# Expert slots of a mixture-of-experts layer on one core: more input buffers, another order of evacuation, and gathers further ahead

## The chip, the core and the metric

The kernel is one program on one core of a Trainium2 chip. It works with TensorE (PE, matrix products and transposes), ScalarE (ACT), VectorE (DVE), GpSimd (POOL) and SyncE (SP, which here only issues transfers). The metric is the device time of one execution in microseconds, the median of several runs.

## What is computed

A block of gated cross-attention (x plus tanh(g) times attention of the normalised x over a context) followed by a gated mixture-of-experts layer, on 2048 tokens of width 512, all in float32. The change touches the second part only:

```python
logits = xt @ router_w + router_b
scores = softmax(logits) + router_bias
# the best two of four groups of experts, and in them the best two of 16 experts
gate = zeros((T, E)).at[arange(T)[:, None], idx].add(vals)

def step(y, p):
    w1, b1, w2, b2, w3, b3, ge = p                 # 512x128, 512x128, 128x512
    h = silu(xt @ w1 + b1) * (xt @ w2 + b2)
    return (y + ge[:, None] * (h @ w3 + b3), None)
y, _ = scan(step, zeros_like(xt), (ew1, eb1, ew2, eb2, ew3, eb3, gate.T))
z = silu(xt @ sw1 + sb1) * (xt @ sw2 + sb2) @ sw3 + sb3     # a shared expert, for all tokens
x = x + tanh(g_ffn) * (y + z)
```

## The kernel before

Products are made from float32 operands split into a high and a low part, each held as fp32r: `three_pass` (lines 82 to 86) issues high by high, low by high and high by low. So each operand is first rounded to its high part on ScalarE and then subtracted into its low part on VectorE.

The three stages run one after the other: keys, values and normalised tokens; attention; the mixture of experts. In the third, each token goes to two experts only. The pairs of token and expert are sorted by expert into **slots** of 256 rows of one expert; there are at most 31 of them (`SLOTS`), and all 31 are run, whether they are filled or not. For slot s:

- SyncE loads the expert's weights into `w_raw[s % 2]` (`load_w`, lines 1522 to 1532): w1 and w2 (L1530), then w3 (L1532). It waits until the low parts of slot s-2 are made from that buffer, then reads the expert's number.
- GpSimd gathers the slot's 256 rows of the normalised x into `rows_in[s % 2]`, in two indirect transfers (`gather`, L1608), and later scatters its 256 rows of output from `y_out[s % 2]` to memory in two more (`scatter`, L1618). Its order is written out without a loop: gather s, then scatter s-4. Before the gather of slot s it waits for the transposes of s-2, before a scatter for `y_out`. Rows of empty places are skipped by a bounds check.
- TensorE's order in slot s (`slot`, in the tensor block) is: transpose the rows of slot s+1 (L2033); the product `up` of slot s, 24 matmuls of 256 columns into `ps_up`; the product `down` of slot s-1, 6 matmuls of 512 columns into `ps_down`.
- ScalarE's order in slot s: xs_hi of s+1 (L1696, two halves), the high part of w1 and w2 of s+1 (L1702), silu of s (L1728), h_hi of s (L1733), `evacuate` of s-1 (L1717: two halves of `ps_down`, scaled by the gate, into `y_out`), the high part of w3 of s+1 (L1708). Each half of `evacuate` waits for its product and for the scatter of s-3, which read the same `y_out`.
- VectorE's order in slot s: xs_lo of s+1 (L1902), the low part of w1 and w2 of s+1 (L1907), a copy of the two columns of biases of s+1 into `biases` (L1909), whose end is the signal `w_up_lo_made` for `up`; then h_sb of s (L1925: `up` plus bias, times silu), h_lo of s (L1928), the low part of w3 of s+1 (L1914).

`over_slots` (lines 1457 to 1465) runs slots 0 to 3 as straight code, slots 4 to 27 in a loop with two slots in its body, and the last three as straight code. SyncE, ScalarE, VectorE and TensorE go through it; GpSimd has no loop.

Around the slots: the shared expert's `up` products run before them and its `down` products after them. Buffers are placed by hand, some on top of others: `x_hi` and `x_lo`, which the shared expert's `up` reads, share their memory with buffers used after it. When the last scatter has landed, the 16 blocks of expert outputs are loaded back (`y2`, L1541) into buffers that are free by then, `rows_in` and `w_raw` among them, added, and stored.

Of the kernel before, what the change touches and what calls it, by code (L numbers as in the profile page):

```python
# [42 lines left out]
E = 16  # L43
# [23 lines left out]
def f32(ap):  # L67

    return ap.bitcast(F32)
# [370 lines left out]


# [773 lines left out]
def stage_three(nc, a, common, scratch, out):  # L1215
# [12 lines left out]
    with ExitStack() as stack:  # L1228
        b = Buffers(nc, stack)
        with ExitStack() as after_up:  # L1230
            e = Buffers(nc, after_up)
            h = []
            for o in range(OCTETS):
# [22 lines left out]
        biases = [b.sb(f"biases{i}", [P, 2]) for i in range(2)]  # L1256
# [20 lines left out]
        w_raw = [b.sb(f"w3_raw{i}", [P, 3, 512]) for i in range(2)]  # L1277
        rows_in = [b.sb(f"rows_in{i}", [P, 2, D]) for i in range(2)]
# [87 lines left out]
        y2_pairs += [buf[:, 0:2] for buf in (*rows_in, *w_raw)]  # L1366
# [48 lines left out]
        x_in = [b.sem(f"slot_x_in{i}") for i in range(2)]  # L1415
        w_in = [b.sem(f"slot_w_in{i}") for i in range(2)]
# [39 lines left out]

        def over_slots(eng, slot):
# [44 lines left out]
        def _(sp):  # L1502
# [19 lines left out]
            def load_w(s, r):  # L1522
                if late(s, 2):

                    sp.wait_ge(w_up_lo_made, s - 1)
                    sp.wait_ge(w_down_lo_made, s - 1)
                column = slice(s, s + 1) if isinstance(s, int) else bass.ds(s, 1)
                e = sp.value_load(moe["slot_expert"][0:1, column], min_val=0, max_val=E - 1)
                for i, name in enumerate(("L0_ffn_ew1", "L0_ffn_ew2")):
                    sp.dma_start(w_raw[r][:, i].rearrange("p (c n) -> p c n", c=C),  # L1530
                                 a[name][e].rearrange("(p c) n -> p c n", c=C)).then_inc(w_in[r], 16)
                sp.dma_start(w_raw[r][:, 2], a["L0_ffn_ew3"][e]).then_inc(w_in[r], 16)  # L1532
# [16 lines left out]
        def _(pool):  # L1549
# [52 lines left out]
            def gather(s):  # L1602
                r = s % 2
                if s >= 2:

                    pool.wait_ge(turned, 2 * s - 2)
                for half in range(2):
                    pool.indirect_dma_start(  # L1608
                        out=rows_in[r][:, half], out_offset=None, in_=xn,
# [524 lines left out]
```

## Time and profile before

| | us |
|---|---|
| median of 3 runs | 1537.16 |
| lowest and highest | 1534.63, 1537.56 |
| the profiled execution, its own time | 1544.32 |
| its span, first to last instruction | 1542.6 |
| busy in the span: PE | 1470.0 |
| DVE | 973.8 |
| ACT | 779.0 |
| POOL | 188.0 |

The profile records one execution. The page gives for each engine the busy time and the number of instructions. Other views are tables of busy time in chosen stretches, groups of instructions by line, sums of waits, and timelines of one engine. L1702 is line 1702 of the kernel; L84 to L86 are the three lines of `three_pass`, so its products are told apart by their tiles: `bank<-xs_hi,w_hi` is `up`, `bank<-w_hi,h_hi` is `down`. In a timeline the columns are start, duration (of all, where several are merged as x2), engine, line, operation, tiles, and, in brackets, how long the engine stood idle before it and what released it. "issue" is a release that the profile can't put down to another engine's signal, "remote" one by an unknown sender. Durations of neighbouring ScalarE and VectorE instructions overlap a little, so start to next start is the time that one costs. A group of lines gives busy time and mean ns of one, then idle time before the group and its releasers.

### The profile page before, as it was taken

The page shows a single profiled execution, that of the slowest core. Times are in us where ns is not written, and L with a number is a line of the kernel's source. Part 1 is how long each engine was busy: PE and PEld are TensorE (multiplying, and loading weights), DVE is VectorE, ACT ScalarE, POOL GpSimd, SP SyncE. Part 2 cuts the span into 40 slices and gives each one's busy share as a digit, 9 for nine tenths or more (in the row PEclk, how much of TensorE's full clock was granted, in tenths as well). Part 3 has the DMA queues.
Part 4 walks back from the last instruction along what each step waited for, and adds up shares of the span by engine and source line. Part 5 has one row for each costly group of instructions (what it writes and reads, how often), then busy time and mean ns, then how long its engine had stood idle before and what let it go on. Part 6 is the DMA issues. An engine that isn't in the chain of part 4 may idle for free.

```text
span 1542.6 us, 26300 instructions
## 1 busy us (share of the span) xinstructions
PE 1470.0 (95%) x9136; PEld 1306.0 (85%) x9136; DVE 973.8 (63%) x1632; ACT 779.0 (50%) x2028; POOL 188.0 (12%) x198
## 2 busy tenths in 40 slices
PE   7999988999999999999999999999999999888986
PEld 5888878999999999989999989999998778887874
DVE  5322237666677666666766657776666778666657
ACT  3112216555566555555655546555555545676760
POOL 0000000000000000000000000000003423677750
PEclk9999999999999999999999999999999999999998
DMA  7576542111223111132211122221110303677528
GB/s 233 162 228 168 138 163 96 48 63 54 68 76 109 64 42 48 66 107 69 74 50 69 41 70 76 82 90 42 48 49 15 110 29 110 226 239 251 162 83 327
DMA packets 97447, 163.67 MB, mean 106 GB/s; under 512 B 12435, under 2 KB 47287, under 8 KB 93258
## 3 DMA queue, kind: packets, MB, share of 16 engines
q1 hardware_dynamic: 87370, 145.62, 29.0%
q0 software_dynamic: 9984, 16.82, 3.3%
q8 instruction: 58, 0.95, 0.2%
q14 instruction: 35, 0.29, 0.1%
HBM read 128.29 MB, written 49.81 MB: 115 GB/s over the span
## 4 chain that ended last, share of the span: by engine, by line
PE 69%; issue 6%; DVE 4%; ACT 2%; SPq 2%; DMA 1%; another core or an unknown queue 1%; ACTq 0%; DVEq 0%
PE ps_q L84 8%; PE ps_q L86 8%; PE ps_q L85 8%; PE ps_y L85 8%; PE ps_y L84 8%; PE ps_y L86 8%; PE ps_s L1008 5%; PE ps_p L1048 4%; PE ps_o L84 2%; PE ps_s L1010 2%; PE ps_o L86 2%; PE ps_o L85 2%; PE bank L84 1%; PE bank L86 1%; PE bank L85 1%
## 5 line engine op out<-in xcount | busy, mean ns | idle before, releaser
L84 PE MATMUL ps_q<-xt,wq_hi 128*128 128x256 f32 x1024 | 302.6, 295 | 4.4 <-PEq L118 4.4
L86 PE MATMUL ps_q<-xt,wq_hi 128*128 128x256 f32 x1024 | 291.7, 285 | 0.0
L85 PE MATMUL ps_q<-xt,wq_lo 128*128 128x256 f32 x1024 | 291.7, 285 | 0.0
L842 ACT ACTIVATE s_sb<-s_sb,nmax 128x128 f32<-128x128 f32 x512 | 199.9, 392 | 129.7 <-DVE nmax L924 129.7
L922 DVE TENSOR_TENSOR s_sb<-ps_s,s_cross 128x512 f32<-128x512 f32 x128 | 88.4, 691 | 232.4 <-ACT s_cross L831 232.2
L831 ACT ACTIVATE s_cross<-ps_s 128x512 f32<-128x512 f32 x128 | 76.5, 597 | 272.3 <-PE ps_s L1010 272.3
L84 PE MATMUL ps_y<-wo_hi,o_hi 128*128 128x512 f32 x512 | 202.3, 395 | 0.9 <-DVE y L902 0.9
L86 PE MATMUL ps_y<-wo_lo,o_hi 128*128 128x512 f32 x512 | 202.6, 396 | 0.0
L85 PE MATMUL ps_y<-wo_hi,o_lo 128*128 128x512 f32 x512 | 202.6, 396 | 0.0
L84 PEld LDWEIGHTS ps_q<-xt,wq_hi 128*128 128x128 f32 x1024 | 196.9, 192 | 5.0 <-issue 4.8
L85 PEld LDWEIGHTS ps_q<-xt,wq_lo 128*128 128x128 f32 x1024 | 197.1, 193 | 0.0
L86 PEld LDWEIGHTS ps_q<-xt,wq_hi 128*128 128x128 f32 x1024 | 196.7, 192 | 0.0
L1008 PE MATMUL ps_s<-kt,q_hi 128*128 128x256 f32 x512 | 125.9, 323 | 9.2 <-issue 7.2
L532 POOL TENSOR_TENSOR trial<-root 128x9 f32<-128x9 f32 (+1 forms) x6 | 1.2, 198 | 961.5 <-DVE root L554 961.2
L84 PEld LDWEIGHTS ps_y<-wo_hi,o_hi 128*128 128x128 f32 x512 | 96.2, 188 | 25.4 <-issue 2.6
L85 PEld LDWEIGHTS ps_y<-wo_hi,o_lo 128*128 128x128 f32 x512 | 96.6, 189 | 23.2
L86 PEld LDWEIGHTS ps_y<-wo_lo,o_hi 128*128 128x128 f32 x512 | 96.1, 188 | 22.6
L1010 PE MATMUL ps_s<-kt,q_lo 128*128 128x128 f32 x512 | 115.0, 225 | 0.0
L1008 PEld LDWEIGHTS ps_s<-kt,q_hi 128*128 128x128 f32 x512 | 97.2, 190 | 15.9 <-issue 8.1
L1010 PEld LDWEIGHTS ps_s<-kt,q_lo 128*128 128x128 f32 x512 | 98.2, 192 | 5.4
L850 ACT ACTIVATE o_hi<-ps_o 128x512 fp32r<-128x512 f32 x128 | 76.9, 601 | 40.7 <-PE ps_o L86 40.7
L842 ACT ACTIVATION_READ_ACCUMULATOR s_sb<-s_sb,nmax 128x1 f32 x512 | 95.9, 187 | 0.0
(262 smaller groups left out, 3230.3 us busy)
## 6 DMA issues: line engine op xcount, KB each, us to landing
xt<-x_scratch SPq DMA_DIRECT2D x32, 1024.0 KB, 4.9
w_raw<-in_L_ffn_ew SPq DMA_DIRECT2D x93, 256.0 KB
v_full<-v_out SPq DMA_DIRECT2D x64, 128.0 KB, 2.6
k_full<-k_out SPq DMA_DIRECT2D x16, 512.0 KB, 2.8
w_raw<-in_L_xattn_Wq SPq DMA_DIRECT2D x16, 512.0 KB, 5.1
kt_raw<-k_full SPq DMA_DIRECT2D x32, 256.0 KB, 2.6
vt_raw<-v_full SPq DMA_DIRECT2D x32, 256.0 KB, 2.7
w_raw<-in_L_xattn_Wo SPq DMA_DIRECT2D x16, 512.0 KB, 4.3
```

The costliest lines, as they stand in the source:

```text
L84: pe.matmul(out, w_hi, x_hi, start=first, stop=False)
L85: pe.matmul(out, w_lo, x_hi, start=False, stop=False)
L86: return pe.matmul(out, w_hi, x_lo, start=False, stop=last)
L532: then(pool.tensor_tensor(w, r, r, ALU.mult))
L831: act.activation(s_cross[:], ps_s[:, :, 1], ACT.Copy).then_inc(cross_copied, 1)
L842: last = act.activation(s_sb[:, i], s_sb[:, i], ACT.Exp, bias=nmax[:, i:i + 1], accum_out=sums[:, i:i + 1])
L850: act.activation(o_hi[s.last_parity][:, :, s.last_token], ps_o[:], ACT.Copy).then_inc(o_hi_made, 1)
L922: dve.tensor_tensor(s_sb[:], ps_s[:, :, 0], s_cross[:], ALU.add).then_inc(folded, 1)
L1008: pe.matmul(ps_s[:, i], q_hi[quad_parity][:, batch, heads].rearrange("p h t -> p (h t)"), k[:, :, batch], start=True, stop=False)
L1010: last = pe.matmul(ps_s[:, i, 0], q_lo[quad_parity][:, batch, heads].rearrange("p h t -> p (h t)"), k[:, 0, batch], start=False, stop=True)
L1048: last = pe.transpose(ps_p[:, i], p_sb[:, i], ident[:])
```

## The change

It does five things, all in the third stage:

1. `AHEAD = 4` buffers for raw weights and for gathered rows, instead of two. The new buffers lie where the shared expert's inputs lay; so the load of slots 2 and 3 waits for the shared expert's `up`, and GpSimd clears the two new row buffers after it has seen six of the eight of those products. `y_out`, the split weights, xs, silu and h keep two buffers.
2. SyncE's load of slot s waits for the low weights of slot s-4; the wait for those of w3 moves to just before the load of w3.
3. GpSimd issues the gathers of slots 2 and 3 ahead, a gather waits for the transposes of slot s-4, and the scatter behind the gather of slot s is that of s-6 (`LAG`), not s-4.
4. ScalarE evacuates slot s-1 right behind silu of slot s, ahead of h_hi.
5. silu and h_sb read their bias from the table `slot_bias` by the slot's column; the copy into `biases` goes, and `w_up_lo_made` comes from the subtraction itself. The loop's body holds four slots; slots 0 to 3 and 28 to 30 are straight code.

```diff
+AHEAD = 4
+LAG = 6
...
-                    e.sb("apart5", [P, 3 * 512])
+                    w_raw = [e.sb("w3_raw2", [P, 3, 512])]
                 if o == 2:
-                    e.sb("apart6", [P, T])
+                    rows_in = [e.sb(f"rows_in{i}", [P, 2, D]) for i in range(2, AHEAD)]
+                if o == 3:
+                    w_raw.append(e.sb("w3_raw3", [P, 3, 512]))
...
         def over_slots(eng, slot):
 
-            for s in range(4):
-                slot(s, s % 2)
-            with eng.Fori(2, LAST // 2 - 1) as k:
-                slot(2 * k, 0)
-                slot(2 * k + 1, 1)
-            for s in range(LAST // 2 * 2 - 2, SLOTS):
-                slot(s, s % 2)
+            for s in range(AHEAD):
+                slot(s, s)
+            with eng.Fori(1, SLOTS // AHEAD) as k:
+                for q in range(AHEAD):
+                    slot(AHEAD * k + q, q)
+            for s in range(SLOTS // AHEAD * AHEAD, SLOTS):
+                slot(s, s % AHEAD)
...
-            def load_w(s, r):
-                if late(s, 2):
-
-                    sp.wait_ge(w_up_lo_made, s - 1)
-                    sp.wait_ge(w_down_lo_made, s - 1)
...
+            def load_w(s, q):
+                if late(s, AHEAD):
+
+                    sp.wait_ge(w_up_lo_made, s - 3)
+                elif s >= 2:
+
+                    sp.wait_ge(shared.up_done, 4 * s - 4)
+                e = sp.value_load(moe["slot_expert"][0:1, one(s)], min_val=0, max_val=E - 1)
...
+                if late(s, AHEAD):
+                    sp.wait_ge(w_down_lo_made, s - 3)
+                sp.dma_start(w_raw[q][:, 2], a["L0_ffn_ew3"][e]).then_inc(w_in[q], 16)
...
             def gather(s):
-                r = s % 2
-                if s >= 2:
-
-                    pool.wait_ge(turned, 2 * s - 2)
+                q = s % AHEAD
+                if s >= AHEAD:
+
+                    pool.wait_ge(turned, 2 * s - 6)
...
             for s in range(2):
                 gather(s)
+            pool.wait_ge(shared.up_done, 6)
+            for q in range(2, AHEAD):
+                pool.memset(rows_in[q][:], 0.0).then_inc(consts_made, 1)
+            pool.wait_ge(consts_made, CONSTS + 3)
+            for s in range(2, AHEAD):
+                gather(s)
             pool.wait_ge(slots_made, 3)
-            for s in range(2, SLOTS + 4):
+            for s in range(AHEAD, SLOTS + LAG):
                 if s < SLOTS:
                     gather(s)
-                if s >= 4:
-                    scatter(s - 4)
+                if s >= LAG:
+                    scatter(s - LAG)
...
-                act.activation(silu[r], ps_up[r][:, 0], ACT.Silu, bias=biases[r][:, 0:1]).then_inc(silu_made, 1)
+                act.activation(silu[r], ps_up[r][:, 0], ACT.Silu, bias=moe["slot_bias"][:, 0, one(s)]
+                               ).then_inc(silu_made, 1)
+                if late(s, 1):
+                    evacuate(s - 1, 1 - r)
 
                 act.wait_ge(h_made, s + 1)
                 if late(s, 2):
                     act.wait_ge(down_done, 2 * s - 2)
                 act.activation(h_hi[r], h_sb[r], ACT.Copy).then_inc(h_hi_made, 1)
-                if late(s, 1):
-                    evacuate(s - 1, 1 - r)
...
-                dve.tensor_tensor(w_lo[r][:, 0:2], w_raw[r][:, 0:2], f32(w_hi[r][:, 0:2]), ALU.subtract)
-                column = slice(s, s + 1) if isinstance(s, int) else bass.ds(s, 1)
-                dve.tensor_copy(biases[r][:], moe["slot_bias"][:, :, column].rearrange("p i a -> p (i a)")
-                                ).then_inc(w_up_lo_made, 1)
...
+                dve.tensor_tensor(w_lo[r][:, 0:2], w_raw[q][:, 0:2], f32(w_hi[r][:, 0:2]), ALU.subtract
+                                  ).then_inc(w_up_lo_made, 1)
...
-                dve.scalar_tensor_tensor(out=h_sb[r], in0=ps_up[r][:, 1], scalar=biases[r][:, 1:2], in1=silu[r],
+                dve.scalar_tensor_tensor(out=h_sb[r], in0=ps_up[r][:, 1], scalar=moe["slot_bias"][:, 1, one(s)], in1=silu[r],
                                          op0=ALU.add, op1=ALU.mult).then_inc(h_made, 1)
```

The rest of the diff passes the buffer's number q through to the readers of `w_raw` and `rows_in` and adapts the counts of their semaphores.

## Rows read from the trace of the kernel before

**Rows 1.** The page: busy us, share of the span and instructions of each engine.
```profile
PE 1470.0 (95%) x9136; PEld 1306.0 (85%) x9136; DVE 973.8 (63%) x1632; ACT 779.0 (50%) x2028; POOL 188.0 (12%) x198
```
**Rows 2.** Busy us by stretch: PE, PEld, DVE, ACT, POOL, PE clock, DMA share, GB/s.
```profile
1306.80:1502.00 195.20, 172.69 (x1169) 154.31 (x1169) 124.63 (x215) 138.12 (x247) 129.62 (x115) 1.00 0.60 194
1502.00:1542.60 40.60, 25.16 (x109) 20.04 (x107) 30.14 (x32) 0.02 (x1) 2.96 (x3) 0.86 0.84 310
```
**Rows 3.** Timeline of TensorE, slots 1 to 4 and slot 30.
```profile
1312.93 0.39 PE L84 MATMUL bank<-xs_hi,w_hi 128*128 128x256 f32 x1 [0.70 <-DVE biases L1909]
...
1317.30 1.12 PE L2033 MATMUL bank<-ident,rows_in 128*128 128x128 f32 x8
1318.18 0.36 PE L84 MATMUL bank<-xs_hi,w_hi 128*128 128x256 f32 x1
...
1329.77 1.22 PE L2033 MATMUL bank<-ident,rows_in 128*128 128x128 f32 x8 [1.86 <-issue]
...
1494.26 0.39 PE L84 MATMUL bank<-xs_hi,w_hi 128*128 128x256 f32 x1 [1.50 <-DVE biases L1909]
...
1497.24 0.40 PE L84 MATMUL bank<-w_hi,h_hi 128*128 128x512 f32 x1
```
**Rows 4.** Groups by line, 1306.8 to 1502.0.
```profile
L1928 DVE TENSOR_TENSOR h_lo<-h_sb,h_hi 128x256 fp32r<-128x256 f32 x31 | 13.3, 428 | 16.0 <-ACT h_hi L1733 10.7 <-issue 5.3
L1733 ACT ACTIVATE h_hi<-h_sb 128x256 fp32r<-128x256 f32 x31 | 13.0, 418 | 34.3 <-issue 16.3 <-DVE h_sb L1925 12.6 <-remote 4.8
...
L1909 DVE COPY biases<-slot_bias 128x2 f32 (+1 forms) x30 | 4.7, 158 | 0.0
```
**Rows 5.** Timeline of ScalarE: slot 3, slots 23 to 25, the last evacuation.
```profile
1328.37 1.06 ACT L1702 ACTIVATE w_hi<-w_raw 128x1024 fp32r<-128x1024 f32 x1 [1.62 <-DMA w_raw<-in_L_ffn_ew]
...
1453.33 1.08 ACT L1696 ACTIVATE xs_hi<-bank 128x512 fp32r<-128x512 f32 x2
...
1459.12 1.08 ACT L1696 ACTIVATE xs_hi<-bank 128x512 fp32r<-128x512 f32 x2
...
1462.67 0.48 ACT L1728 ACTIVATE silu<-bank,biases 128x256 f32<-128x256 f32 x1 [1.52 <-remote]
...
1465.83 1.08 ACT L1696 ACTIVATE xs_hi<-bank 128x512 fp32r<-128x512 f32 x2
...
1500.75 1.27 ACT L1717 ACTIVATE y_out<-bank,slot_gate 128x512 f32<-128x512 f32 x2 [0.64 <-DMA slots_y<-y_out,slot_row]
```
**Rows 6.** Timeline of VectorE.
```profile
1424.52 1.23 DVE L1907 TENSOR_TENSOR w_lo<-w_raw,w_hi 128x1024 fp32r<-128x1024 f32 x1 [0.88 <-ACT w_hi L1702]
...
1456.63 0.47 DVE L1925 SCALAR_TENSOR_TENSOR h_sb<-bank,biases,silu 128x256 f32<-128x256 f32 x1
...
1459.26 0.69 DVE L1914 TENSOR_TENSOR w_lo<-w_raw,w_hi 128x512 fp32r<-128x512 f32 x1 [1.25 <-issue]
```
**Rows 7.** Waits summed, 1306.8 to 1502.0: total us, times, longest.
```profile
ACT silu L1728 <- remote: 16.1, 12, 2.3
```
**Rows 8.** Timeline of GpSimd.
```profile
1320.30 1.33 POOL L1618 DMA_INDIRECT slots_y<-y_out,slot_row  x1 [4.47 <-ACT y_out L1717]
...
1323.24 1.05 POOL L1608 DMA_INDIRECT rows_in<-xn_table,slot_token  x1 [0.30 <-issue]
...
1326.06 1.35 POOL L1618 DMA_INDIRECT slots_y<-y_out,slot_row  x1 [0.44 <-issue]
...
1424.96 1.70 POOL L1608 DMA_INDIRECT rows_in<-xn_table,slot_token  x1 [0.30 <-issue]
...
1459.51 1.35 POOL L1618 DMA_INDIRECT slots_y<-y_out,slot_row  x1 [0.46 <-issue]
...
1496.97 1.32 POOL L1618 DMA_INDIRECT slots_y<-y_out,slot_row  x1 [3.41 <-ACT y_out L1717]
...
1500.88 0.98 POOL L1618 DMA_INDIRECT slots_y<-y_out,slot_row  x1 [1.30 <-ACT y_out L1717]
```
**Rows 9.** Timeline of SyncE's queue.
```profile
1322.00 0.83 SPq L1530 DMA_DIRECT2D w_raw<-in_L_ffn_ew  x2
```

More of the change, by code:

```diff
@@ L1255, in stage_three @@
         }
-        biases = [b.sb(f"biases{i}", [P, 2]) for i in range(2)]
+        b.sb("apart8", [P, 4])
         with ExitStack() as up_front:
@@ L1275, in stage_three @@
         sw_down = [[b.sb(f"sw_down_{part}0", [P, 512], F32R) for part in ("hi", "lo")]]
-        w_raw = [b.sb(f"w3_raw{i}", [P, 3, 512]) for i in range(2)]
-        rows_in = [b.sb(f"rows_in{i}", [P, 2, D]) for i in range(2)]
+        w_raw = [b.sb(f"w3_raw{i}", [P, 3, 512]) for i in range(2)] + w_raw
+        rows_in = [b.sb(f"rows_in{i}", [P, 2, D]) for i in range(2)] + rows_in
         sw_raw = w_raw
@@ L1365, in stage_three @@
             y2_pairs = y2_early + [e.sb(f"y2_{k}", [P, 2, D])[:] for k in range(10)]
-        y2_pairs += [buf[:, 0:2] for buf in (*rows_in, *w_raw)]
+        y2_pairs += [buf[:, 0:2] for buf in (*rows_in[0:2], *w_raw[0:2])]
         y2 = [y2_pairs[2 * p:2 * p + 2] for p in range(TILES // 2)]
@@ L1413, in stage_three @@
         gates_lo_made = b.sem("gates_lo_made")
-        x_in = [b.sem(f"slot_x_in{i}") for i in range(2)]
-        w_in = [b.sem(f"slot_w_in{i}") for i in range(2)]
+        x_in = [b.sem(f"slot_x_in{i}") for i in range(AHEAD)]
+        w_in = [b.sem(f"slot_w_in{i}") for i in range(AHEAD)]
         turned = b.sem("slot_turned")
@@ L1718, in evacuate, with slot @@
                                    scale=moe["slot_gate"][:, c]).then_inc(y_out_made, 1)
-            def slot(s, r):
+            def slot(s, q):
+                r = q % 2
                 if not (isinstance(s, int) and s == LAST):
                     xs_high(s + 1, 1 - r)
-                    w_up_high(s + 1, 1 - r)
+                    w_up_high(s + 1, (q + 1) % AHEAD)
                 act.wait_ge(up_done, s + 1)
@@ L1903, in xs_low, with w_up_low, w_down_low, slot @@
                                       ALU.subtract).then_inc(xs_lo_made, 1)
-            def w_up_low(s, r):
+            def w_up_low(s, q):
+                r = q % 2
                 dve.wait_ge(w_up_hi_made, s + 1)
-                dve.tensor_tensor(w_lo[r][:, 0:2], w_raw[r][:, 0:2], f32(w_hi[r][:, 0:2]), ALU.subtract)
-                column = slice(s, s + 1) if isinstance(s, int) else bass.ds(s, 1)
-                dve.tensor_copy(biases[r][:], moe["slot_bias"][:, :, column].rearrange("p i a -> p (i a)")
-                                ).then_inc(w_up_lo_made, 1)
-            def w_down_low(s, r):
+                dve.tensor_tensor(w_lo[r][:, 0:2], w_raw[q][:, 0:2], f32(w_hi[r][:, 0:2]), ALU.subtract
+                                  ).then_inc(w_up_lo_made, 1)
+            def w_down_low(s, q):
+                r = q % 2
                 dve.wait_ge(w_down_hi_made, s + 1)
-                dve.tensor_tensor(w_lo[r][:, 2], w_raw[r][:, 2], f32(w_hi[r][:, 2]), ALU.subtract
+                dve.tensor_tensor(w_lo[r][:, 2], w_raw[q][:, 2], f32(w_hi[r][:, 2]), ALU.subtract
                                   ).then_inc(w_down_lo_made, 1)
-            def slot(s, r):
+            def slot(s, q):
+                r = q % 2
                 if not (isinstance(s, int) and s == LAST):
                     xs_low(s + 1, 1 - r)
-                    w_up_low(s + 1, 1 - r)
+                    w_up_low(s + 1, (q + 1) % AHEAD)
                 if late(s, 2):
@@ L2023, in _, with turn @@
                 shared.pe_up(pe, 6, part)
[L2025 removed]
+            def turn(s, q):
                 for half in range(2):
                     if half == 0:
[L2029 removed]
+                        pe.wait_ge(x_in[q], 8 * (s - q) + 32)
                     if late(s, 1):
@@ L2032, in turn @@
                     for c in range(C):
-                        last = pe.transpose(ps_t[half][:, c, :], by_part(rows_in[r][:, half], c), ident[:])
+                        last = pe.transpose(ps_t[half][:, c, :], by_part(rows_in[q][:, half], c), ident[:])
                     last.then_inc(turned, 1)
@@ L2058, in down, with slot @@
                                w_lo[r][:, 2], True, True).then_inc(down_done, 1)
-            def slot(s, r):
+            def slot(s, q):
+                r = q % 2
                 if not (isinstance(s, int) and s == LAST):
-                    turn(s + 1, 1 - r)
+                    turn(s + 1, (q + 1) % AHEAD)
                 up(s, r)
```

30 lines of the change are left out of this document (15 added, 15 removed).

## The prediction

> **What bounds the kernel now.** I read the page first: TensorE is busy 95% of the span [rows 1], so a gain must come from a stretch where it is not. The table by stretches shows one: of the 195.2 us in which the 31 expert slots run (1306.8 to 1502.0), TensorE is busy 172.7, ScalarE 138.1, GpSimd 129.6, VectorE 124.6 [rows 2]. Nobody is full, so what counts is the chain inside a slot. The diff changes nothing outside this stretch except two clears and the time of a few transfers.
>
> The stretch opens with slot 0's first product, that of slot 30 starts at 1494.26 [rows 3]: 187.5 us for 30 slots, 6.25 each. TensorE can do better: slot 1 starts at 1312.93, slot 2 at 1318.18, right behind the transposes begun at 1317.30 [rows 3]. So 5.25 is its floor, and 1 us a slot, 30 in all, is waiting.
>
> ScalarE's timeline shows for what. It rounds transposed rows (xs_hi) and weights, does silu, then stands for h_sb (34.3 us before h_hi, 1.1 a slot [rows 4]), and only then rounds h and evacuates the slot before. From xs_hi to xs_hi this is 5.79 (1453.33 to 1459.12 [rows 5]), the fast kind of slot. VectorE makes it wait: it is at the weights and the copy of the biases, and starts h_sb at 1456.63 [rows 6]. In the other kind silu comes 1.52 late, released by what the profile calls remote, and xs_hi to xs_hi is 6.71 (1459.12 to 1465.83) [rows 5]. That stands once in each pass of the two-slot loop: 12 waits, 16.1 us [rows 7]. Two smaller losses lie at the head: weights 1.62 late at 1328.37 [rows 5], and TensorE idle 1.86 before the transposes at 1329.77 [rows 3], whose gather was issued only at 1323.24, behind slot 0's scatter, which had stood 4.47 for y_out [rows 8].
>
> **Part by part.** *Evacuation behind silu.* ScalarE's own work is 138.1/31 = 4.5 a slot [rows 2]. The evacuation now fills the wait for h_sb. What is late next: it needs the last product of the slot before, which runs behind this slot's first one and takes 5.25 less 2.98 (1494.26 to 1497.24) less 0.88 (the transposes), 1.4 [rows 3]. So it ends about 2.1 after the first product, and h_hi starts about 1 us later than today. Its reader, the next last product, comes a whole first product later (2.98); that hides it except in slot 30, where nothing lies between: 0.8 is added there. Queued behind the moved waits on ScalarE are h_hi, the down weights and xs_hi, on VectorE h_lo and its part of the weights; at 5.3 a slot I find 1 us of slack for all. ScalarE's cycle falls from 5.79 below TensorE's floor.
>
> *Biases read in place.* 30 copies of 0.158 go [rows 4]. The two readers take a register step more in a loop: 0 to 0.1 a slot, less than the copy. Once ScalarE no longer bounds, this is worth 0; at most 4.7.
>
> *Four raw buffers.* A weight load takes 6.4 (issued at 1322.00 [rows 9], its reader released at 1328.37 [rows 5]) and goes out after the low weights of two slots before. Two slots more take the waits away. SyncE's third copy waits for the down weights, with only its own later loads behind it. The loads of slots 2 and 3 go out earlier and meet the first gathers: 0, at worst 1 us.
>
> *Passes of four slots.* Six instead of twelve. If the late silu belongs to a pass, six go, each worth 6.71 less 5.79, 0.92, less what slack absorbs. Bounds: 5.5 us gained, or 0 if each pair of slots keeps it.
>
> *GpSimd.* A slot costs it two scatters and two gathers; this doesn't shrink. Gaps are 0.30 and free lengths 0.98 (1500.88) to 1.05 (1323.24), so a free cycle is 4 x 1.01 + 4 x 0.30 = 5.24 [rows 8]. But lengths depend on VectorE: the gather at 1424.96, begun inside the weights' subtraction (1424.52 to 1425.75), took 1.70, the scatter at 1459.51, begun inside the smaller one (1459.26 to 1459.95), 1.35 [rows 6, 8]. In both the length is what was left of VectorE's instruction plus 0.91. So a start that falls into one of its instructions on SBUF operands (1.23, 0.69 and 0.43 a slot [rows 4, 6]) waits for its end, less the 0.08 that a free one hides. Four starts spread over 5.5 us give 4 x (1.15² + 0.61² + 0.35²)/2/5.5 = 0.66 on average. The cycle is between 5.24 (no hit) and 7.35 (all hit in full); I take 5.8, nearest to what two starts in a row show with one hit, 1320.30 to 1326.06, 5.76 [rows 8].
>
> The Trainium skill (SBUF — State Buffer, Who interferes with whom) says that a VectorE instruction with two SBUF inputs contends with GpSimd's reads and that the loser blocks for the whole instruction, but infers that tensor_tensor leaves the generation of descriptors alone. The 1.70 and 1.35 speak against that inference for indirect transfers; by it the cycle would be 5.24, as in rival 1.
>
> *Gathers ahead.* With four buffers the gather of slot s waits for the transposes of s-4, and the scatter of s-6 comes behind it. Behind slot u's scatter now stands the gather of u+7, not u+5, so the 1.86 goes, and GpSimd may fall two slots behind before a gather is late. The tighter leash is y_out, still two buffers: to evacuate u+2, u's scatter must have landed, 3.8 after its start in a quiet stretch (1496.97 [rows 8], reader released at 1500.75 [rows 5]), up to the load's 6.4 in a busy one. One slot's delay fits, but not a GpSimd that loses 0.5 in each. The two clears come before slot 0; scatter 0 stands 4.47 for y_out today [rows 8], which covers them.
>
> **The sum.** Scatter 0 starts 1 us earlier, at 1319.2. From there GpSimd does 24 pairs: 24 x 5.8 = 139.2, so scatter 24 starts at 1458.4, has landed at 1462.2, and slot 26 is evacuated at 1463.5 (1.27 [rows 5]). By then the gathers are done, GpSimd catches up, and four slots follow at 5.4: 1485.1; with 0.8 for the last slot 1485.9, against 1502.0. Of these 16 I take off 1 for worse phases with fuller transfer engines (share 0.60 today [rows 2]): 15 us. The tail (40.6 us [rows 2]) stays: its loads start when the last scatter has landed. The profiled execution took 1544.3, its span 1542.6; after, 1529.3. It lies 7.2 above the median of 1537.16, and this carries over: 1522.
>
> **Rivals.**
> 1. TensorE bounds. GpSimd's starts fall between VectorE's instructions, or its slack is enough. Slot 30 starts at 1312.8 + 29 x 5.25 + 7 x 0.92 = 1471.5 and is evacuated 8.6 later (7.8 today and 0.8): 1480.1, gain 22, 1515; without the late silus 28, 1509. For it: slot 1 ran so. Against: 1.35s stand in nearly every slot.
> 2. Partly used. The late silu stays in every second slot and delays evacuation and h_hi with it: 6.0 a slot. 30 x 0.25 less 0.8 gains 7: 1530. For it: its cause isn't in the profile. The Trainium skill (Runtime: NRT & Kernel Launch, Instruction fetch mechanics) has a taken branch stall for a fetch when its target has left the window; by that a doubled body stalls once a pass or, once outgrown, more often. The rows show one late silu a pass, not its cause.
> 3. It doesn't do what it says: something unseen (the remote release) holds TensorE at 6.25, and waits only change their name: 1537.
> 4. Slower: GpSimd's starts hit VectorE's instructions in full. h_hi now stands behind an evacuation that stands behind a scatter's landing, so the whole chain follows GpSimd. At a cycle of 7.0: 1319.2 + 168 + 3.8 + 1.3 + 21.6 + 0.8 = 1514.7, 12.7 later, 1550. It decides from a cycle of 6.5 on: (1502.0 - 0.8 - 21.6 - 5.1 - 1319.2)/24. Against: 5.76 today.
>
> **Chances.** Forecast (gain 10 to 19) 0.47; rival 1 0.20; rival 2 0.15; rival 3 0.07; rival 4 0.11. About 0.2%, 3 us, is what a measurement of this kernel can tell from no change. Faster 0.82, same 0.07, slower 0.11. The range runs from 1512 (rival 1, between its values) to 1535 (rival 2 with little left).
>
> **What would show it.** Slots' first products 5.7 to 5.9 apart up to slot 26, then about 5.4; GpSimd's gaps at 0.30 nearly throughout, none at 0.44 or more; ScalarE's waits before y_out put down to the scatter's transfer, none before h_hi, none for w_raw; half as many remote waits. If GpSimd still idles for y_out and slots are 5.4 apart, rival 1 holds; if the idle time before silu stays at 16 us, rival 2. Wrong altogether if scatters take 1.7 and more.

## The result and the profile after

| | us |
|---|---|
| before, median of 4 | 1536.89 (1534.63 to 1537.56) |
| after, median of 4 | 1524.38 (1523.96 to 1525.0) |
| ratio | 0.9921, 95% interval 0.9905 to 0.9937 |
| after, the profiled execution | 1524.43, its span 1522.7 |

The change gains 12.5 us; 1522 was predicted, with a range of 1512 to 1535. That lies close, but two steps on the way were off by more than the difference, in opposite directions, so the closeness of the number is in part luck. The rest of the text is mostly about these steps. Below, one execution of rows2 (1793.11) and one of the kernel before beside before_again (1791.31) ran at a granted clock of 0.75 and are left out of the medians.

The page of after, engines, and the two stretches that answer to [rows 1, 2]:

```profile
PE 1463.0 (96%) x9136; PEld 1305.5 (86%) x9136; DVE 970.9 (64%) x1601; ACT 778.1 (51%) x2028; POOL 192.3 (13%) x200
```

```profile
1306.50:1482.00 175.50, 165.37 (x1170) 154.21 (x1169) 121.51 (x185) 137.60 (x248) 131.07 (x114) 1.00 0.67 211
1482.00:1522.70 40.70, 25.32 (x109) 20.17 (x107) 30.16 (x32) 0.00 (x0) 1.96 (x2) 0.88 0.84 310
```

The slots take 175.5 where they took 195.2, the tail is unchanged. TensorE's timeline at the head (start, length, instruction, idle time before it), to be read against [rows 3]:

```profile
1312.61 0.39 PE L84 MATMUL bank<-xs_hi,w_hi 128*128 128x256 f32 x1 [0.62 <-DVE w_lo L1930]
...
1316.98 1.12 PE L2056 MATMUL bank<-ident,rows_in 128*128 128x128 f32 x8
1317.86 0.37 PE L84 MATMUL bank<-xs_hi,w_hi 128*128 128x256 f32 x1
...
1323.07 0.36 PE L84 MATMUL bank<-xs_hi,w_hi 128*128 128x256 f32 x1
```

First products now follow each other at TensorE's floor, 5.21 to 5.25, for eight intervals from slot 1 (1312.61) to slot 9 (1354.37). From there to slot 27 (1458.80) they are 5.80 apart on average, singly between 5.21 and 6.92, then 5.21 again, and 4.34 before slot 30. Groups of instructions and waits show who holds the middle part:

```profile
L1737 ACT ACTIVATE y_out<-bank,slot_gate 128x512 f32<-128x512 f32 x62 | 40.2, 686 | 30.2 <-DMA slots_y<-y_out,slot_row 24.9 <-PE bank L86 5.2
L1757 ACT ACTIVATE h_hi<-h_sb 128x256 fp32r<-128x256 f32 x31 | 12.8, 413 | 1.6 <-DVE h_sb L1948 1.5
L1951 DVE TENSOR_TENSOR h_lo<-h_sb,h_hi 128x256 fp32r<-128x256 f32 x31 | 13.3, 428 | 45.1 <-ACT h_hi L1757 45.1
```

ScalarE's 34.3 us before h_hi [rows 4] are 1.6. In their place it waits 24.9 us, in 16 slots, for the landing of the scatter before it may write y_out again. GpSimd issues without a pause: between scatter 0 and scatter 24 no gap on it is above 0.31. VectorE's timeline and, below it, GpSimd's:

```profile
1339.69 0.69 DVE L1936 TENSOR_TENSOR w_lo<-w_raw,w_hi 128x512 fp32r<-128x512 f32 x1
1340.30 1.28 DVE L1924 TENSOR_TENSOR xs_lo<-bank,xs_hi 128x512 fp32r<-128x512 f32 x2
1341.61 1.23 DVE L1930 TENSOR_TENSOR w_lo<-w_raw,w_hi 128x1024 fp32r<-128x1024 f32 x1
```

```profile
1337.69 1.00 POOL L1630 DMA_INDIRECT slots_y<-y_out,slot_row  x1 [0.30 <-issue]
1338.99 1.04 POOL L1620 DMA_INDIRECT rows_in<-xn_table,slot_token  x1 [0.30 <-ACT y_out L1737]
1340.34 1.01 POOL L1620 DMA_INDIRECT rows_in<-xn_table,slot_token  x1 [0.31 <-issue]
1341.66 2.08 POOL L1630 DMA_INDIRECT slots_y<-y_out,slot_row  x1 [0.31 <-issue]
1344.05 1.00 POOL L1630 DMA_INDIRECT slots_y<-y_out,slot_row  x1 [0.30 <-issue]
```

The scatter at 1341.66 begins 0.05 behind the start of VectorE's long subtraction and takes 2.08: the 1.18 that were left of it plus 0.90, the rule read from [rows 6, 8]. The gather at 1340.34 begins 0.04 before the end of the smaller subtraction and inside xs_lo, which reads one operand from PSUM; it takes 1.01. Scatter 0 starts at 1318.69, scatter 24 at 1459.76: 24 cycles of 5.88.

```profile
1318.69 1.03 POOL L1630 DMA_INDIRECT slots_y<-y_out,slot_row  x1 [3.17 <-ACT y_out L1737]
...
1459.76 1.03 POOL L1630 DMA_INDIRECT slots_y<-y_out,slot_row  x1 [0.30 <-issue]
```

Of the late silus [rows 7] there is none left. In the sum of waits silu has one releaser:

```profile
ACT silu L1749 <- PE bank L86: 5.0, 11, 1.4
```

### The profile page after: what moved, and what is told of

It is laid out like the page before. It is cut to its first block, busy times and chain, and to the rows that moved or that the text cites. A ratio compares the mean times of both kernels' runs of the same rounds, so it can differ in the third digit from the quotient of the medians.

```text
span 1522.7 us, 26170 instructions
## 1 busy us (share of the span) xinstructions
PE 1463.0 (96%) x9136; PEld 1305.5 (86%) x9136; DVE 970.9 (64%) x1601; ACT 778.1 (51%) x2028; POOL 192.3 (13%) x200
## 4 chain that ended last, share of the span: by engine, by line
PE 72%; DVE 4%; issue 4%; POOL 3%; DMA 2%; ACT 1%; ACTq 0%; POOLq 0%; DVEq 0%
PE ps_q L84 8%; PE ps_q L86 8%; PE ps_y L85 8%; PE ps_q L85 8%; PE ps_y L86 8%; PE ps_y L84 8%; PE ps_s L1012 5%; PE ps_p L1052 4%; PE ps_o L84 2%; PE ps_s L1014 2%; PE bank L84 2%; PE ps_o L86 2%; PE ps_o L85 2%; PE bank L86 2%; PE bank L85 2%
```

## The experiments

A time here is the median of a kernel; ratios are to the kernel before on the same chip. Chip 9 matters for the reading: there the kernel before took 1547.9 (31 executions, 1543.0 to 1551.55), on the others 1535 to 1537. So I compare on one chip first, and use the silu intervals of the traces besides. "30 slots" is the time from silu 0 to silu 30, "silu remote" the idle time before silus that the profile puts down to an unknown sender, and in how many slots. These are read from one trace for each kernel. evac_back to yout4 ran on chip 1, b_pass4 to split_sub on chip 9, the next three on chip 15, before_again on chip 6.

| kernel | time | ratio (95%) | before beside it | 30 slots | silu "remote" |
|---|---|---|---|---|---|
| evac_back | 1526.94 | 0.9947 (0.9926 to 0.9968) | 1535.02 | 169.6 | none |
| rows2 | 1524.35 | 0.993 (0.991 to 0.995) | 1535.02 | 166.7 | none |
| one_gather | 1513.35 | 0.9857 (0.9841 to 0.9874) | 1535.02 | 154.9 | none |
| yout4 | 1516.65 | 0.9877 (0.9861 to 0.9894) | 1535.02 | 157.3 | none |
| b_pass4 | 1546.08 | 0.9991 (0.9979 to 1.0004) | 1547.9 | 188.9 | 19.8 in 11 |
| b_evac | 1554.44 | 1.0051 (1.0032 to 1.0071) | 1547.9 | 197.0 | 42.4 in 14 |
| bias_back | 1545.63 | 0.9983 (0.9968 to 0.9998) | 1547.9 | 187.7 | 43.1 in 14 |
| split_sub | 1552.64 | 1.0036 (1.0024 to 1.0047) | 1547.9 | 194.7 | 44.2 in 13 |
| after_again | 1522.67 | 0.9921 (0.9894 to 0.9949) | 1536.27 | 163.2 | none |
| bias_back2 | 1524.95 | 0.9922 (0.9902 to 0.9942) | 1536.27 | 166.4 | none |
| split_inc | 1518.21 | 0.9879 (0.9857 to 0.99) | 1536.27 | 157.9 | none |
| before_again | 1537.31 | 1.0001 (0.9985 to 1.0017) | 1535.33 | 178.3 | none |

The changed kernel's own first trace has 165.5, that of before behind the prediction 186.0 (with 16.1 in 12).

**What is the bound: GpSimd, ScalarE, or something behind both?** First the evacuation, put back behind h_hi:

```diff
-                if late(s, 1):
-                    evacuate(s - 1, 1 - r)
                 act.activation(h_hi[r], h_sb[r], ACT.Copy).then_inc(h_hi_made, 1)
+                if late(s, 1):
+                    evacuate(s - 1, 1 - r)
```

> The changed kernel with the evacuation of slot s-1 put back behind h_hi, all else as changed. Theory A (ScalarE's wait for h_sb set the pace of the quiet slots before, GpSimd sets that of the loaded ones now): the first nine slots go back from 5.22 to about 5.8 us each, the later ones stay at 5.8 because GpSimd needs that anyway: 9 x 0.57 = 5 us slower than the changed kernel, 1529, and the idle time before h_hi is 30 us again. Rival 1 (the whole gain hangs on this move): 1537. Rival 2 (the gain came from the gathers ahead, the move is worth nothing): 1524.

Theory A holds in the trace: from slot 1 to slot 29, silus are 5.64 to 5.80 apart, 5.72 mostly. That is the ring, the closed chain of ScalarE's work in one slot and its wait for h_sb, and ScalarE stands for h_sb in every slot:

```profile
ACT h_hi L1755 <- DVE h_sb L1948: 41.1, 31, 1.4
...
ACT y_out L1737 <- DMA slots_y<-y_out,slot_row: 0.7, 1, 0.7
```

The time, 2.6 over the changed kernel's (4.0 by the ratios), is less than the 5 expected; the intervals of the two overlap. 169.6 against 163.2 and 165.5 for the 30 slots is the clearer sign. Rival 1 falls: of the gain against before, 8.1 remain on this chip without this move.

Then GpSimd relieved of one transfer in four. From slot 4 on this kernel leaves out the second gather of a slot, and that half of the rows keeps what was there before:

```diff
-                for half in range(2):
+                for half in range(2 if s < AHEAD else 1):
                     pool.indirect_dma_start(
```

> The changed kernel in which from slot 4 on only the first of a slot's two gathers is issued (the second half of the rows keeps what was there): GpSimd's work a slot falls from four indirect transfers to three. Theory A (GpSimd's four transfers, 5.8 us a slot with the hits by VectorE, bound slots 9 to 27): its cycle is now about 4.4, below TensorE's 5.22, all slots run 5.22 apart: 18 x 0.58 = 10 us faster, 1514, and ScalarE's 24.9 us of waiting for the scatter before y_out falls below 5. Rival (the waits for the scatter are a shadow, TensorE's or ScalarE's chain or the load on the transfer engines sets 5.8): 1522 or more.

1513.35 for 1514. Silus are 5.12 to 5.38 apart from slot 1 to slot 29, and scatters 5.22. In the waits no line has y_out standing for a scatter; GpSimd stands for y_out instead:

```profile
L1630 POOL DMA_INDIRECT slots_y<-y_out,slot_row x62 | 61.8, 997 | 54.6 <-ACT y_out L1737 45.2 <-issue 9.5
```

So GpSimd's four transfers a slot are what bounds the changed kernel from slot 9 on, and taking one of them away leaves TensorE's floor. A gather less is also less load on the transfer engines, but the load isn't the cause: yout4, below, keeps slots at 5.22 from 1330 to 1400 with these engines busy to 0.89, where the changed kernel has 0.86. With the leash lengthened in place of the work:

```diff
-        y_out = [b.sb(f"y_out{i}", [P, 2, D]) for i in range(2)]
+        y_out = [b.sb(f"y_out{i}", [P, 2, D])[:] for i in range(2)] + y2_early[0:2]
...
-                    if late(s, 2):
-                        act.wait_ge(y_scattered[r], 16 * (s - r))
+                    if late(s, 4):
+                        act.wait_ge(y_scattered[q], 8 * (s - q))
```

The rest of its diff gives y_out two semaphores more, which other stages share from then on, and writes out ScalarE's first eight slots.

> The changed kernel with four buffers for y_out in place of two (two of the tail's early buffers serve), so that the evacuation of slot u waits for the scatter of u-4 and not of u-2; ScalarE's first eight slots are written out. Theory A (GpSimd loses some 0.6 us a slot against TensorE over 18 slots, 10.8 us in all, and two buffers more allow it 10.4 more): slots run 5.2 to 5.3 apart to the end, GpSimd catches up when the gathers are over, 8 to 10 us faster, 1515. Rival 1 (gathers now come late instead, since GpSimd does the same work in the same order): TensorE waits for transposed rows from about slot 15 on, 2 to 5 us faster, 1520. Rival 2 (y_out is a shadow): 1524.

7.7 us below the changed kernel, between theory A and rival 1, and the trace has both: silus 5.15 to 5.38 apart up to slot 23, then 5.90, 5.15, 5.61, 5.73, 5.42, 5.73, where gathers come late. GpSimd works at the same pace as before (scatter 0 to scatter 24 in 24 x 5.86); the products only run ahead of it.

**What do the gathers ahead bring?**

```diff
-LAG = 6
+LAG = 4
...
-                q = s % AHEAD
-                if s >= AHEAD:
-                    pool.wait_ge(turned, 2 * s - 6)
+                q = s % 2
+                if s >= 2:
+                    pool.wait_ge(turned, 2 * s - 2)
```

> The changed kernel with the gathers as in the kernel before: two row buffers, gather s waits for the transposes of s-2, scatter s-4 behind it. Theory A (GpSimd's head start of two slots is what lets slots 1 to 9 run at 5.22; late silus belonged to the evacuation or to the passes): silu's idle time stays below 4 us, the quiet slots at the head shrink to some five, 2 to 4 us slower, 1527. Rival (the late silus of the kernel before came with gathers that land only just before their transposes): silu is released late by remote 12 times or more, some 16 us of idle time, 12 x 0.92 = 11 us slower, 1535.

1524.35 is the changed kernel's 1524.38, and the ratios are 0.993 and 0.9921 with intervals that overlap: no loss that can be told. The waiting changes its name only. Here it is TensorE that waits, for gathered rows before it transposes them, and ScalarE hardly for the scatter:

```profile
PEld bank L2050 <- issue: 14.9, 18, 1.7
PE bank L2050 <- DMA rows_in<-xn_table,slot_token: 7.6, 10, 1.3
...
ACT y_out L1731 <- DMA slots_y<-y_out,slot_row: 0.4, 1, 0.4
```

Gathers that land just before their transposes bring no late silu here. What settles the rival are bias_back and split_sub, below: they have the four row buffers and late silus all the same.

**Single edits, on chip 9, where the kernel before takes 1548.** Two of the next four put one edit into the kernel before, one takes one out of the changed kernel, and the fourth cuts VectorE's long subtraction. b_pass4, in the kernel before:

```diff
-            with eng.Fori(2, LAST // 2 - 1) as k:
-                slot(2 * k, 0)
-                slot(2 * k + 1, 1)
+            with eng.Fori(1, SLOTS // 4) as k:
+                for q in range(4):
+                    slot(4 * k + q, q % 2)
```

> The kernel before with passes of four slots in place of two, all else as before. Theory A (the 12 late silus come from the form of the two-slot pass itself, for the changed kernel has none of them even with its evacuation put back or with two row buffers): all are gone, the silus stand 5.72 us apart as in the changed kernel with the evacuation put back, not 6.21 on average as before: 24 x 0.49 = 11.8 us faster than before, 1523. Theory B (the prediction's: one for each pass): half remain, 6 us faster, 1529. Rival (they come from the two weight buffers or from the copy of the biases): 12 remain, 1535.

b_evac, in the kernel before:

```diff
+                if late(s, 1):
+                    evacuate(s - 1, 1 - r)
                 act.wait_ge(h_made, s + 1)
...
-                if late(s, 1):
-                    evacuate(s - 1, 1 - r)
```

> The kernel before with the evacuation moved behind silu, all else as before. Theory A (late silus belong to the two-slot pass and stay): one slot in two is late, the wait for h_sb is filled, slots come 6.0 apart, 7 us faster than before, 1528. Rival 1 (late silus disappear with the move, GpSimd bounds): 1524. Rival 2 (silu's lateness comes through ScalarE itself, the move is worth nothing): 1535.

bias_back, in the changed kernel:

```diff
-                act.activation(silu[r], ps_up[r][:, 0], ACT.Silu, bias=moe["slot_bias"][:, 0, one(s)]
+                act.activation(silu[r], ps_up[r][:, 0], ACT.Silu, bias=biases[r][:, 0:1]
...
+                dve.tensor_copy(biases[r][:], moe["slot_bias"][:, :, one(s)].rearrange("p i a -> p (i a)")
+                                ).then_inc(w_up_lo_made, 1)
```

> The changed kernel with VectorE's copy of the biases put back. Theory A (VectorE has slack, GpSimd sets the pace): no difference that can be measured, 1524.5, silu without late releases. Rival 1 (late silus come with the copy): silu idle by remote 5 us or more, 1530. Rival 2 (the copy delays the start of each first product by its 0.16 us): up to 30 x 0.16 = 4.7 slower, 1529.

split_sub, in the changed kernel:

```diff
-                dve.tensor_tensor(w_lo[r][:, 0:2], w_raw[q][:, 0:2], f32(w_hi[r][:, 0:2]), ALU.subtract
-                                  ).then_inc(w_up_lo_made, 1)
+                for i in range(2):
+                    last = dve.tensor_tensor(w_lo[r][:, i], w_raw[q][:, i], f32(w_hi[r][:, i]), ALU.subtract)
+                last.then_inc(w_up_lo_made, 1)
```

> The changed kernel with VectorE's subtraction for the up weights (128x1024, 1.23 us) cut into two of 128x512 (0.69 each). Theory A (an indirect transfer of GpSimd that begins inside a VectorE instruction on SBUF operands waits for the end of that one instruction): no length over about 1.65 where the changed kernel has 1.8 to 2.1; the mean delay a slot falls from 4 x (1.15^2 + 0.61^2 + 0.35^2)/2/5.5 = 0.66 to 0.49, 24 x 0.17 = 4 us faster than the changed kernel, 1520. Rival 1 (GpSimd gets its turn only when VectorE goes idle, two instructions back to back hold it for both): lengths up to 2.1 and more, the mean not smaller, 1525. Rival 2 (VectorE's 0.15 us more a slot reaches TensorE): 1528.

The times expected were for chips on which the kernel before takes 1535, so only the ratios can be held against them. b_pass4 stays level with the kernel before and keeps 11 late silus, as its rival had it. The other three come out slower than under any of their theories: b_evac was at worst to be worth nothing and is 0.5% slower than the kernel before; bias_back and split_sub were at worst to stay 0.4 and 0.6% faster than it, and are 0.2% faster and 0.4% slower. split_sub's transfers are as theory A wanted, none in the slots above 1.56. All four have late silus, also the two that come from the changed kernel, with up to 5.3 us before one silu. The timelines of split_sub around the longest show what is late. TensorE ends the product that this silu reads by 1433.6, does the last product of the slot before, the transposes (1434.81), and is in the next slot's first product when silu starts:

```profile
1433.30 0.28 PE L86 MATMUL bank<-xs_lo,w_hi 128*128 128x256 f32 x1
...
1434.81 1.12 PE L2057 MATMUL bank<-ident,rows_in 128*128 128x128 f32 x8
1435.69 0.36 PE L84 MATMUL bank<-xs_hi,w_hi 128*128 128x256 f32 x1
...
1438.67 0.38 PE L85 MATMUL bank<-xs_hi,w_lo 128*128 128x256 f32 x1 [0.42 <-issue]
```

```profile
1432.46 1.06 ACT L1721 ACTIVATE w_hi<-w_raw 128x1024 fp32r<-128x1024 f32 x1
1438.79 0.47 ACT L1749 ACTIVATE silu<-bank,slot_bias 128x256 f32<-128x256 f32 x1 [5.27 <-remote]
```

The product is on time by its records, the signal of its end is 5 us late. This is more than a reading of the name "remote", for the trace also keeps when each semaphore was raised. The one that tells silu of the product is raised 0.30 behind the start of the product's last matmul in each of slots 1 to 30 of the changed kernel, and of before_again too. In split_sub it is so in 18 of these slots; in the other twelve, slots 3, 5, 7 and so on to 25, it comes 2.0 to 5.37 behind that start. In the slot shown it is raised at 1438.67, and the signals of the two halves of the last product and of the two transposes behind it follow within 0.22. So ScalarE wasn't slow to see the signal. Nor was the work itself that late, for it lasts more than 2 us and can't have ended all within 0.22: TensorE's signals were held back together. The profile says "remote" since it finds no instruction that ended just then.

b_pass4 takes theory A and theory B of its text away: with passes of four slots the lateness still falls on about every second slot. Slot 3, late by this in split_sub, is straight code there, not in a loop at all. The two edits of the changed kernel left two theories, that VectorE's additional instruction does it, or the chip.

**Kernel or chip?** The changed kernel and bias_back, both unaltered, on one chip, and beside them split_inc, in which both halves of the cut subtraction signal:

```diff
+                for i in range(2):
+                    dve.tensor_tensor(w_lo[r][:, i], w_raw[q][:, i], f32(w_hi[r][:, i]), ALU.subtract
+                                      ).then_inc(w_up_lo_made, 1)
```

> The changed kernel itself once more, unaltered, to stand beside the next two on one chip. Open is why two small edits of it (the copy of the biases put back; the up weights' subtraction cut in two) brought the late silus back, some 44 us of idle time released by remote, and took 1546 and 1553. Theory K (it lies in the kernels: in both, and in the kernel before, VectorE has one instruction more a slot, which signals nothing): this run has no late silu, whatever the chip, and about 1524. Theory C (it lies in the chip or the day of that call, on which the kernel before took 1548 and not 1535): if the kernel before takes 1545 or more here, this run has late silus too and takes over 1535; if it takes 1535, neither this run nor the next two have any.

> The changed kernel with the copy of the biases put back, once more unaltered, beside the changed kernel itself on one chip. Theory K (VectorE's additional instruction brings the late silus): silu idle by remote over 15 us, at least 8 us slower than the changed kernel. Theory C (the chip or the day did): the same time as the changed kernel within 2 us, and the same count of late silus.

> The changed kernel with the up weights' subtraction cut in two as before, but now both halves signal (the semaphore counts two a slot, its readers wait for two). Theory K1 (what brings the late silus is a VectorE instruction in the slot that signals nothing): none here, and by shorter hits of GpSimd 1 to 4 us faster than the changed kernel, 1521. Theory K2 (one more VectorE instruction a slot, signalling or not): late silus, 1535 to 1553. Theory C (the chip): late silus exactly if the changed kernel has them here.

Theory C: the same kernel takes 1545.63 on chip 9 and 1524.95 on chip 15, with 43.1 us of late silus in one trace and none in the other. Theories K, K1 and K2 are dead. Whether it is the chip or the time of these runs isn't shown, since nothing was measured on chip 9 at another time. The last run asks the same of the kernel before:

> The kernel before itself once more, unaltered, for its trace in a run near its median. Open is how much of the changed kernel's gain comes from late silus that are gone. Theory N (the late silus belong to single chips or executions, like those of the kernel with the biases' copy, which had 44 us of them on one chip and none on another; the profiled execution before, 7 us over its median, had them by that chance): where this run takes about 1536 it has no late silu, silu's idle time by remote is below 2 us, silus stand about 5.79 apart nearly everywhere, and the 30 slots take 174 to 178 us. Theory S (they belong to the kernel before wherever it runs, and passes of four slots or the gathers' head start took them away): 10 or more late silus, 16 us of idle time, silus alternately 7.4 and 5.1 apart, 186 us for the 30 slots.

Theory N in the main. Its profiled execution took 1537.67 (span 1535.9), has no late silu, and its 31 waits for h_sb come one in each slot. The 30 slots take 178.3, just above the 174 to 178 expected, and its silus are 5.7 to 5.9 apart in about half of the slots only; some of the others wait for weights, and TensorE for rows:

```profile
ACT h_hi L1733 <- DVE h_sb L1925: 42.6, 31, 1.5
...
PEld bank L2033 <- DVE xs_lo L1902: 6.3, 8, 1.0
...
ACT w_hi L1702 <- DMA w_raw<-in_L_ffn_ew: 3.7, 6, 1.6
```

```profile
1307.80:1495.40 187.60, 171.14 (x1170) 155.47 (x1170) 123.58 (x215) 137.03 (x248) 129.92 (x115) 0.99 0.63 203
1495.40:1535.90 40.50, 25.10 (x108) 19.98 (x107) 30.14 (x32) 0.00 (x0) 2.96 (x3) 0.87 0.84 311
```

The slots take 187.6 here and took 195.2 in [rows 2]. The difference, 7.6, accounts for the 7.2 by which the execution behind the prediction lay above the median. This trace has a chance loss of its own: in slot 1 TensorE ran at the lower of its two clock levels, 1.2 GHz, up to 1317.19 (matmuls 0.21 apart, then 0.12), and the slot took 1.4 longer than in [rows 3]. TensorE had stood idle for 0.69 before; in [rows 3] it had for 0.70, with no such fall. The stretch, with the granted clock third from the end:

```profile
1313.90:1318.60 4.70, 4.57 (x25) 4.57 (x26) 4.09 (x8) 2.85 (x5) 2.52 (x2) 0.64 0.37 96
```

**Do shorter VectorE instructions help GpSimd?** split_inc took 1518.21 beside 1522.67 for the changed kernel. The intervals of the ratios just overlap (0.99 and 0.9894), but of the eight executions of the changed kernel one, at 1518.96, lies below split_inc's highest, 1519.0. Groups of GpSimd's transfers (busy us, mean ns), first after_again, then split_inc:

```profile
L1630 POOL DMA_INDIRECT slots_y<-y_out,slot_row x62 | 68.2, 1100 | 29.3 <-issue 16.7 <-ACT y_out L1737 12.6
L1620 POOL DMA_INDIRECT rows_in<-xn_table,slot_token x53 | 61.1, 1152 | 17.2 <-issue 15.0 <-PE bank L2056 1.3 <-ACT y_out L1737 0.9
```

```profile
L1630 POOL DMA_INDIRECT slots_y<-y_out,slot_row x62 | 66.0, 1064 | 30.0 <-issue 16.3 <-ACT y_out L1737 13.7
L1620 POOL DMA_INDIRECT rows_in<-xn_table,slot_token x55 | 58.8, 1068 | 18.6 <-issue 14.7 <-PE bank L2057 2.4 <-ACT y_out L1737 1.5
```

Two halves back to back do not hold GpSimd for both: the longest transfer from slot 1 on is 1.55 (2.08 in the changed kernel), the cycle 5.53 (5.77 in after_again, 5.88 in the first trace). Four transfers, each shorter by the difference of the means above, give the 0.24 between 5.77 and 5.53. Both split_inc and yout4 are faster than the changed kernel; the two together weren't run.

## Why the prediction came out right, and where its steps were wrong

**What bounds the kernel: half wrong.** The wait for h_sb is there in every slot and is the bound of the kernel before. The second kind of slot, with silu 1.5 late and 6.71 long, was read as the kernel's [rows 5, 7]. It was that execution's: before_again doesn't have it. Where nothing else is late there, ScalarE's ring is 5.79, or 5.87 over a pass's end; with the waits for weights and rows and slot 1's clock it is 5.94 on average (178.3/30).

**Evacuation behind silu: right in kind.** ScalarE fell below TensorE's floor, h_sb's wait went, VectorE stands behind h_hi (45.1 us) at no cost, and y_out's two buffers are what is late next. Alone it is worth 2.6 us by the medians, not clear of noise, and 4 to 6 by the traces.

**Biases: right, 0 within what was measured.** bias_back2 lies 2.3 above after_again, but single executions spread over 5.4 and 7.7 and the ratios agree. While ScalarE is the bound, the copy may count a little: before_again's ring is 5.79, evac_back's 5.72, but these two kernels differ in more than the copy.

**Raw buffers: counted at 0, rightly in a sum that GpSimd bounds.** The waits went: 3.7 us in 6 slots before, none after. Going back to two raw buffers alone wasn't run.

**Passes: the step failed.** "If the late silu belongs to a pass, six go." None belonged to a pass (b_pass4, and slot 3 of split_sub). What a pass's end costs ScalarE is 0.08: one interval in four in evac_back is 5.80 instead of 5.72.

**GpSimd at 5.8: right.** 5.88 and 5.77 in two traces of the changed kernel, from lengths that were read off six rows. The average over chance starts gave 5.24 + 0.66 = 5.90, and 5.8 was taken as nearer to one pair of starts; the average was at least as good. one_gather shows that it is the bound and not a shadow. The 0.5 to 0.6 above the free cycle comes from VectorE's instructions: transfers that begin inside none of its subtractions on two SBUF operands took 0.98 to 1.05 from slot 1 on, and with shorter subtractions the excess shrinks to 0.29 (split_inc). The Trainium skill (SBUF — State Buffer, Who interferes with whom) infers that a tensor_tensor leaves descriptor generation alone; the 2.08 and the effect of the cut speak against this for indirect transfers. The prediction's last sign, "wrong altogether if scatters take 1.7 and more", was set too sharply: three scatters took 2.0 and more, and the forecast held. What came out otherwise besides is the order: products are not 5.7 to 5.9 apart from the start. GpSimd's two slots of slack are used up first, at 5.22 a slot.

**Gathers ahead: right that y_out is the tighter leash, wrong if taken as a gain.** Without them rows2 takes the same time.

**The sum.** Term by term, predicted and measured:

| | predicted | measured |
|---|---|---|
| slot 0's product to scatter 0 | 12.4 | 12.2 |
| 24 cycles of GpSimd | 139.2 | 141.1 |
| scatter 24 to the end of evacuation 26 | 5.1 | 4.8 |
| evacuations 27 to 30 | 22.4 | 17.3 |
| added for worse phases | 1 | 0 |
| the whole | 180.1 | 175.4 |

The mis-sized term is the fourth: "four slots follow at 5.4: 1485.1; with 0.8 for the last slot 1485.9". The evacuations of slots 26 to 30:

```profile
1463.30 1.27 ACT L1737 ACTIVATE y_out<-bank,slot_gate 128x512 f32<-128x512 f32 x2 [0.78 <-PE bank L86]
1467.86 1.39 ACT L1737 ACTIVATE y_out<-bank,slot_gate 128x512 f32<-128x512 f32 x2 [0.18 <-PE bank L86]
1473.08 1.38 ACT L1737 ACTIVATE y_out<-bank,slot_gate 128x512 f32<-128x512 f32 x2 [0.22 <-PE bank L86]
1477.34 1.38 ACT L1737 ACTIVATE y_out<-bank,slot_gate 128x512 f32<-128x512 f32 x2 [0.22 <-PE bank L86]
1480.53 1.38 ACT L1737 ACTIVATE y_out<-bank,slot_gate 128x512 f32<-128x512 f32 x2 [1.51 <-PE bank L86]
```

The steps are 4.56, 5.22, 4.26 and 3.19. Two are short for a plain reason. Slot 30 has no transposes of a next slot in front of it (silu 29 to silu 30 is 4.26), and its own last product follows at once, with no further slot's first product in between. [rows 3] had slot 30 of before, from which this could be read; I put an average slot, and a supplement on top, in its place.

So the profiled span was put 5 us too high: 1527.6, with the 1 us for worse phases counted, against 1522.7. Then 7.2 were taken off, since "this carries over". It did not: the 7.2 were the late silus of that one execution, and the changed kernel's profile lies on its median. 5 too much and 7.2 too little leave 2.4 too little; that the two nearly cancel is luck. The gain was predicted as 15 and is 12.5, or 13.2 between the spans of before_again and after; against the trace I had, it is 19.9. A forecast against the median needed the slots of an ordinary execution, 187.6 in before_again, not 195.2.

**The rivals.** Rival 1, TensorE bounds, is what one_gather makes of the kernel, 1513; rival 3 fell. Rival 2's condition, a silu late in every second slot that delays the evacuation, is met on chip 9, but it costs more than that rival said: there b_evac is slower than the kernel before by 0.5%. It is slower as rival 4 had it, yet not by rival 4's cause, for GpSimd stands 41.7 us for y_out in it and so doesn't set the pace. With silu up to 4.6 late, an evacuation that stands behind it comes late too, and TensorE waits for its bank:

```profile
ACT silu L1728 <- remote: 42.4, 14, 4.6
...
PEld bank L84 <- ACT y_out L1717: 11.9, 9, 1.8
```

**What stays open.** Why TensorE's signals come late in some executions wasn't found; the traces show that neither the pass, the copy, the gathers' distance nor the evacuation's place makes it. The changed kernel itself wasn't run on chip 9. bias_back, which is nearly it, gained 0.2% there, so the 12.5 us hold for executions without late signals only. And of the 12.5 us, 8 to 10 are still there with the evacuation back (8.1 on the chip of evac_back, 9.9 between the medians). rows2 and bias_back2 give up none or little of them, each alone. Worked out from before_again against evac_back (178.3 less 169.6, 8.7): 3.7 for weights, about 2 for 0.07 a slot, 0.5 for six passes' ends, and 1.5 in slot 1, which are the lower clock there and not the change. This division is argued, not shown.

## What to carry to other kernels

Before a stall in a profile is costed, ask whether it belongs to the kernel: a profiled execution 0.5% above the median had a whole kind of wait that an ordinary one hasn't. When the critical chain is shortened, look for the engine with back-to-back issues and gaps that never grow, here GpSimd, and count its work per step with its hits; a longer leash (yout4) or shorter instructions beside it (split_inc) then can pay where further work on the chain wouldn't: 7.7 and 4.5 us here. Cost the last iterations by their own rows.

## What the runs showed of the hardware

- The signal of a finished product can be raised late while TensorE goes on working: 5.37 us behind the start of the product's last matmul where 0.30 is usual (split_sub; the changed kernel). Signals held back come together, five within 0.22 us. The same code had 43.1 us of waits from this on one chip and none on another, for 1545.6 and 1525.0 (bias_back, bias_back2).
- An indirect transfer that starts inside a VectorE subtraction with both operands in SBUF lasts until that one ends, plus 0.9; a second subtraction behind it doesn't prolong this (longest 1.55 with 0.69 instructions, 2.08 with 1.23). One that starts inside an instruction with one operand in PSUM (xs_lo, h_sb) isn't prolonged: 0.98 to 1.05.
- GpSimd's transfers free of this take 0.98 to 1.05 with 0.30 between, from slot 1 on in the traces of after, after_again, split_inc, one_gather and yout4.
- 15 matmuls in a row at the lower clock level, 1.2 GHz (before_again, slot 1; granted clock 0.64 over 1313.9 to 1318.6), cost 1.4 us, after an idle time of 0.69 that left the clock untouched in the trace of before (0.70).
